# Two deformable convolution layers on one core: gathered tile and tent-sampled half strip issued as one mixed step

## What is computed

```
x = x + relu(bn(deform(gn(x))))                        # layer 0
y = gelu(bn1(deform_masked(gn(x))))                    # layer 1, first convolution
x = x + gelu(bn2(deform_masked(y)) + gn(x))            # layer 1, second convolution
```

## Time and profile before

| | us |
|---|---|
| median of 3 runs | 7444.57 |
| lowest and highest of them | 7428.19, 7445.72 |
| the profiled execution | 7424.53 |
| its span, first to last instruction | 7422.6 |
| mean granted clock of TensorE, share of full | 0.848 |

### The profile page before, as it was taken

The page is one execution under the profiler, slowest core; times in us unless marked ns, Lnnn a source line. Parts: engine busy times, 40 slices in busy tenths (PEclk is TensorE's granted clock), DMA queues, the critical chain, the costliest instruction groups (busy, mean ns, idle before and its releaser), DMA issues. The chain is left out here.

```text
span 7422.6 us, 123328 instructions
## 1 busy us (share of the span) xinstructions
PE 5979.6 (81%) x46325; PEld 4693.6 (63%) x46325; DVE 4858.5 (65%) x11223; ACT 2184.1 (29%) x3355; POOL 5073.7 (68%) x4909
## 2 busy tenths in 40 slices
PE   7985665664878887788887788879999998998997
PEld 6874554553666665566665455547777776776775
DVE  7875666664777675677765455556676775676665
ACT  1221222121222222222222222224444443443442
POOL 0007777777777774777774666767777777777776
PEclk9986777775888887888887788879999998998998
DMA  4322333333333332333331222223333333333332
GB/s 143 99 95 87 93 88 91 92 94 93 99 89 98 89 88 71 89 95 97 103 89 56 76 73 65 62 81 87 91 84 95 88 88 88 91 89 76 93 85 72
DMA packets 366225, 653.49 MB, mean 88 GB/s; under 512 B 113896, under 2 KB 272488, under 8 KB 357736
## 3 DMA queue, kind: packets, MB, share of 16 engines
q0 software_dynamic: 156672, 321.18, 16.9%
q1 hardware_dynamic: 209000, 324.67, 14.2%
HBM read 599.42 MB, written 46.07 MB: 87 GB/s over the span
## 5 line engine op out<-in xcount | busy, mean ns | idle before, releaser
L832 POOL DMA_INDIRECT G<-table,IDX x4896 | 5059.6, 1033 | 2302.9 <-issue 2130.8
L1343 ACT ACTIVATE SAMP<-RED 96x384 f32<-96x384 f32 x1216 | 591.0, 486 | 4357.3 <-PE RED L1049 1327.2
L1981 DVE TENSOR_TENSOR ARENA<-ARENA 128x288 f32<-128x288 f32 x3744 | 1440.6, 451 | 216.7 <-PE RED L1049 207.0
L1049 PE MATMUL RED<-IDENT,ARENA 128*96 128x128 f32 x11232 | 1396.0, 286 | 198.8 <-DVE ARENA L1981 198.8
L1049 PEld LDWEIGHTS RED<-IDENT,ARENA 128*96 128x96 f32 x11232 | 1299.3, 133 | 277.3 <-issue 267.2
L1838 DVE TENSOR_TENSOR G<-G,W 128x1152 f32<-128x1152 f32 x476 | 646.8, 1359 | 603.1 <-DMA G<-table,IDX 598.6
L1034 PE MATMUL RED<-IDENT,SUM 128*96 128x128 f32 x1056 | 242.9, 353 | 745.0 <-DVE SUM L1852 745.0
L1151 PE MATMUL BTP<-PAD,ARENA 80*128 x2304 | 756.9, 452 | 66.7 <-DVE ARENA L1831 32.7
L992 PE MATMUL OFFC<-PAD,ARENA 128*54 128x128 f32 (+1 forms) x10944 | 787.8, 305 | 27.2 <-ACT PAD L1252 15.4
L992 PEld LDWEIGHTS OFFC<-PAD,ARENA 128*54 128x54 f32 (+1 forms) x10944 | 704.7, 140 | 95.7 <-issue 74.0
L1089 PE MATMUL BTP<-X 80*128 80x480 f32 x1152 | 694.2, 735 | 6.5 <-DVE X L1942 4.1
(11 more groups left out here) (201 smaller groups left out, 6175.6 us busy)
## 6 DMA issues: line engine op xcount, KB each, us to landing
ARENA<-wtab SPq DMA_DIRECT2D x208, 800.0 KB
G<-table,IDX POOLq DMA_INDIRECT x4896
ARENA<-xo SPq DMA_DIRECT2D x96, 720.0 KB
table<-TB SPq DMA_DIRECT2D x64, 384.0 KB, 2.5
X<-xo SPq DMA_DIRECT2D x64, 360.0 KB, 3.6
X<-x SPq DMA_DIRECT2D x2, 3200.0 KB, 22.5
out<-X SPq DMA_DIRECT2D x20, 320.0 KB
wtab<-TB SPq DMA_DIRECT2D x16, 384.0 KB, 2.8
```

What stands on the lines that cost most here:

```text
L832: pool.indirect_dma_start(G[:, b, k, :], None, tables[seg.table], bass.IndirectOffsetOnAxis(ap=IDX[:, q, b * TAPS + k:b * TAPS + k + 1], a ...
L1049: last = nc.tensor.matmul(RED[b % 2][0:TPG * C, gr * 128:(gr + 1) * 128], PROD[gr][:, sft, :], IDENT[:, :], start=(sft == 0), stop=(sft == ...
L1343: nc.scalar.activation(SAMP[:, x], RED[x][0:TPG * C, 0:GROUPS * 128].rearrange("p (g n) -> p g n", g=GROUPS), ACT.Copy).then_inc(z.samp_re ...
L1981: last = nc.vector.tensor_tensor(out=PROD[gr][:, :, j * C:(j + 1) * C].rearrange("p (dy dx) c -> p dy dx c", dy=3), in0=win[:, gr:gr + 3, ...
```

## The change

A new kind of step, f, holds a gathered tile and a half strip. It replaces every c and the g beside it: 8 steps in pairs 1 and 2 each, 16 in pair 3. `consume_both` writes its order by hand on SP, PE, ACT and DVE; the tile's projections now go unit by unit (`project_units`), the half reduces into `RED[1]` alone and the tile into `RED[0]` alone. `place` is split into `locate` and `index`, which stand apart. `tents1` works on one image at a time and is called in later units of the step ahead. `MIXED_C` now holds 12 g, 6 f and 26 d (it was 19 g, 6 c, 26 d), and three tiles of a pair, in place of two, come after the norm: f, 5 builds, f, 4 builds, g. POOL's program is as it was.

```diff
-MIXED_C = ("gddgddgc" * 2) * 3 + "gdd"
+MIXED_C = "gddgdfd" * 4 + "gddgddfd" * 2
...
+        def mix(on, c, kinds, gseg, at, dseg, at_d, cseg, at_c, then=""):
...
+                halves = at_c + kinds[:i + 1].count("f")
+                ahead = (cseg, halves) if (kinds + then)[i + 1:i + 2] == "f" else None
...
+                if kind == "f":
+                    k = halves - 1
+                    prep = None
+                    if k % 2 and k + 1 < len(cseg.tiles):
+                        prep = (cseg, k // 2 + 1, 0, c.n, cseg.first // 2 + k // 2 + 1)
+                    half = Step(cseg, k, 0, c.u + 1, c.v, 1 - c.u % 2, cseg.first + k, c.n, prep, (), closes, None, c.wg, False, c.built)
+                    on.consume_both(step, half)
+                    before += ((cseg, k, c.u + 1, 1 - c.u % 2),)
+                    c.n += prep is not None
+                    c.half += 1
...
-                    mix(on, c, MIXED_C, g, 0, DSEG[p + 1], 0, s, 0)
+                    mix(on, c, MIXED_C, g, 0, DSEG[p + 1], 0, s, 0, "f")
                     if p == 2:
                         on.dense_done(c.u)
                     on.norm(3 + p, (p + 1) // 2, (p + 1) % 2, None, c.u)
-                    for k in range(2):
-                        mix(on, c, "gc", g, 19 + k, None, 0, s, 6 + k)
-                        builds_of(on, c, WBUILD[k], KB["t", p + 1], GSEG[p + 1], False)
+                    mix(on, c, "f", g, 18, None, 0, s, 6, "f")
+                    builds_of(on, c, WBUILD[0], KB["t", p + 1], GSEG[p + 1], False)
+                    mix(on, c, "f", g, 19, None, 0, s, 7)
+                    builds_of(on, c, WBUILD[1], KB["t", p + 1], GSEG[p + 1], False)
+                    mix(on, c, "g", g, 20, None, 0, s, 8)
                 else:
                     on.finished(ENDS[0])
-                    for k in range(3):
-                        mix(on, c, "gcgc", g, 2 * k, None, 0, s, 2 * k)
+                    for k, kinds in enumerate(("gf", "ff", "ff")):
+                        mix(on, c, kinds, g, 2 * k, None, 0, s, max(0, 2 * k - 1), "f")
                         builds_of(on, c, range(3 * k, 3 * k + 3), KB["t", PAIRS], GSEG[PAIRS], False)
-                    mix(on, c, "gc" * 10 + "g", g, 6, None, 0, s, 6)
+                    mix(on, c, "f" * 11, g, 6, None, 0, s, 5)
...
+                def consume_both(step, half):
+                    if half.prep:
+                        on.prepare(*half.prep)
+                    if half.t + 1 < len(half.seg.tiles):
                         for im in range(2):
...
+                            load_half(half.seg, half.t + 1, im)
...
+                def consume_both(step, half):
                     for e in tb_evac:
                         pe.wait_ge(e, step.built)
...
+                    for side, e in enumerate(xt1_evac):
+                        pe.wait_ge(e, column_evacs(half.seg.p, side))
+                    tiles = [(b, 0, step.po, b // 2) for b in range(UNITS)]
+                    halves = [(im, 1, half.po, 0) for im in range(2)]
+                    on.taps_half(half, 0, 0)
+                    if step.prep:
+                        on.convolve(*step.prep)
+                    on.taps_half(half, 0, 1)
+                    on.reduce_half(half, 0, 0)
+                    if step.prep:
+                        on.turn_offsets(*step.prep)
+                    on.taps_half(half, 0, 2)
+                    on.turn_unit(step, 0)
+                    on.reduce_half(half, 0, 1)
+                    on.taps_half(half, 1, 0)
+                    on.reduce_half(half, 0, 2)
+                    on.project_units(step, tiles[0:1], 3)
+                    on.turn_unit(step, 1)
+                    on.taps_half(half, 1, 1)
+                    on.reduce_half(half, 1, 0)
+                    on.project_units(step, [tiles[1], halves[0]], 5)
+                    if half.prep:
+                        on.convolve_within(*half.prep)
+                    on.taps_half(half, 1, 2)
+                    on.turn_unit(step, 2)
+                    on.reduce_half(half, 1, 1)
+                    on.project_units(step, tiles[2:3], 6)
+                    on.turn_unit(step, 3)
+                    on.reduce_half(half, 1, 2)
+                    if half.prep:
+                        on.turn_after_tile(*half.prep, step.prep)
+                    on.project_units(step, tiles[3:4], 7)
+                    on.project_units(step, halves[1:2], 8)
...
+                def consume_both(step, half):
+                    def tile_sample(b):
+                        act.wait_ge(main.reduced, UNITS * step.i + b + 1 + 2)
+                        on.sample(step.v + (1, 3, 4, 6)[b], 0)
+
+                    def half_sample(im):
                         act.wait_ge(prod_used, step.wg + 3 * im + 3 + GROUPS)
...
+                        on.sample(step.v + (2, 5)[im], 1)
+
+                    if step.prep:
+                        on.offsets(*step.prep)
+                    tile_sample(0)
+                    if step.prep:
+                        on.mask(*step.prep)
+                    half_sample(0)
+                    tile_sample(1)
+                    if half.prep:
+                        on.offsets(*half.prep)
+                    tile_sample(2)
+                    tile_sample(3)
+                    half_sample(1)
+                    if half.prep:
+                        on.mask(*half.prep)
+                    if step.ahead:
+                        on.tents1(*step.ahead, 0)
+                    on.finish(step, 7)
+                    on.finish(half, 8)
+                    if step.ahead:
+                        on.tents1(*step.ahead, 1)
...
+                def consume_both(step, half):
+                    m, q = step.i, step.q
                     dve.wait_ge(main.prep_v, PREP * step.n)
                     for im in range(2):
...
+                        b = 2 * im
+                        on.weight_half(half, im, 0)
+                        on.scale(main, m, q, b)
+                        on.weight_half(half, im, 1)
+                        on.halve(main, m, b)
+                        on.weight_half(half, im, 2)
+                        on.weight_half(half, im, 3)
+                        on.sum_up(main, m, b)
+                        on.weight_half(half, im, 4)
+                        on.scale(main, m, q, b + 1)
+                        on.weight_half(half, im, 5)
+                        if im == 0:
+                            for tile_ in step.before:
+                                on.finish(*tile_)
+                        on.weight_half(half, im, 6)
+                        on.halve(main, m, b + 1)
+                        on.weight_half(half, im, 7)
+                        on.sum_up(main, m, b + 1)
+                        on.weight_half(half, im, 8)
+                        if im == 0 and step.prep:
+                            on.locate(*step.prep)
                     if step.prep:
...
+                        on.index(*step.prep)
+                        on.weigh(*step.prep)
+                    if half.prep:
+                        on.prepare(*half.prep)
                     if step.closes:
...
+                        for now in (step, half):
+                            on.finish(now.seg, now.t, now.u, now.po)
```

More of the change, by code:

```diff
@@ L384, in loop @@
             with eng.Fori(0, count) as j:
-                before = None
+                before = ()
                 for i, slot_ in enumerate(slots):
@@ new lines, in mix @@
+                prep = seg2 and (seg2, t2, buffer_of(seg2, t2), c.n, seg2.first + t2)
+                step = Step(seg, t, buffer_of(seg, t), c.u, c.v, c.u % 2, seg.first + t, c.n, prep, before, closes,
+                            ahead, c.wg, c.drain, c.built)
+                before = ((seg, t, c.u, c.u % 2),)
+                c.n += prep is not None
[7 more added lines that the diff above has]
+                    before += ((cseg, k, c.u + 1, 1 - c.u % 2),)
+                    c.n += prep is not None
+                    c.half += 1
+                elif kind == "d":
+                    on.consume_dense(step)
+                else:
+                    on.consume(step)
@@ L1069, in reduce_half, with turn_unit @@
                                                 start=(w == 0), stop=(w == WY1 - 1), is_transpose=True)
                     last.then_inc(prod_used, 1)
-                def consume_half(step):
-                    seg, t, prep = step.seg, step.t, step.prep
-                    p, h = seg.p, step.i
-                    r0, _ = column_groups(p)
+                def turn_unit(step, b):
+                    pe.wait_ge(main.summed, UNITS * step.i + b + 1 + UNITS)
+                    pe.wait_ge(main.samp_ready, step.v + (1, 3, 5, 6)[b])
+                    for gr in range(GROUPS):
+                        last = nc.tensor.transpose(RED[0][0:TPG * C, gr * 128:(gr + 1) * 128],
```

(28 more changed lines are left out.)

174 lines of the change are left out of this document (74 added, 100 removed).

## The result

The changed kernel takes **7306.56 us** in the median of 4 runs (7298.02 to 7324.67), the kernel before 7442.59 (4 runs, 7428.19 to 7445.72). The ratio is **0.9824**, with a 95% interval of 0.9801 to 0.9848: 136 us less, where the forecast said 198. The time lies 7 us outside the forecast's own 7200 to 7300 and inside the full range, 7190 to 7370. The profiled execution took 7298.0 us, span 7296.2.

What follows compares the result with a forecast made beforehand. POOL's gather issue was taken as nearly the limit, its 265 us of waits the most to gain. Savings of 157 us before pair 3 plus 55 in pair 3, less 14 at the end, gave 198: 7247 us, range 7190 to 7370.

Steps and rivals of the forecast that it cites:

- f's price, 38 and 42 us: Time of a step f: 38 us plain, 42 where its half prepares the next strip, mean 40, in place of 49.2.
- the rivals with f at 47 and 52: PE waits inside f and its clock falls: f at 47 gives 7363, chance 0.2; at 52 gives 7525, chance 0.09.
- One of their signs: Signs of the slow-f rivals: f steps over 46 us apart, DVE waiting for BTP, and a clock under 0.8.
- Pair 1, norm at 2757.7: In pair 1 the norm's first instruction moves from 2822.2 to 2757.7, 64.5 us less.
- The 6 us allowed for two limits that don't mesh: Added in pairs 1 and 2, where engines and POOL were forecast as equal limits: 6 us of loss each.
- The passage, 120: From the norm's first instruction to the next pair's first gather: parts sum to 119, taken as 120, in place of 132.8.
- Pair 2, 1058 from norm to norm: From pair 1's norm to pair 2's: 1058 us in place of 1136.9, 79 less.
- Pair 3, 45.8 us per tile: POOL's gathering sets pair 3's tiles: 45.8 us each, 782 us in place of 837, 55 less.
- The end, 14 us: Behind pair 3's last gather, the last unit must land and four weightings follow before X is reloaded: 14 us lost.
- The clock: Dense tiles run at granted clock 1.00, against the skill's transpose rule; by that rule f takes 60, kernel some 340 slower.
- The step that failed: In the bound: gathers keep 1118, 1058 and 968 ns in pairs 1 to 3, so POOL's 265 us of waits cap the gain.
- The third rival: Gathers get longer in pairs 1 and 2 because SP's dense windows come closer together: 80 us given back, 7327; chance 0.11.

Runs made afterwards that it cites:

- bursts: Changed kernel, but inside f DVE scales, halves and sums both units of an image in one burst behind its second weighting; 7312.02 us, ratio 0.9862.
- neither instruction: Changed kernel with DVE's scaling and halving of every unit left out, SP's loads kept; 27294.81 us on another chip, including gathers of the general path.
- each part alone: Kernel before with three tiles kept and no f: 7388.88 us. Changed kernel with f but only two tiles kept: 7324.21 us.

## Why the prediction was right, and where it was short

The time lies in the range, on its slower side, and the mechanism was the one forecast: POOL's waits went, and POOL's own issue became the limit. That the forecast's own 7200 to 7300 was missed has one main cause, at the end of this part.

- *f's price, 38 and 42 us.* 38 is right, and if anything high. With two tiles kept the passage ends with the wait for the table; its 116.9 us, less the other parts of the forecast's sum (43), leave 36.9 for each f. The 42 of an f that prepares a strip was not met where the engines set the time. Ahead of the tile beside the norm POOL waits 1.7 us in pair 1 and 4.6 in pair 2 for a unit, and never over 0.3 in pair 3, so f bounds none of them. The clock did not fall (0.86 in pairs 1 and 2, 0.85 in pair 3): the rivals with f at 47 and 52 are out. One of their signs came all the same: in pair 3 the steps are 47.3 us apart, and DVE waits longer for BTP than for G (us in total, times, longest). With POOL never waiting there, f's own waits are no bound.

```profile
DVE ARENA L2031 <- PE BTP L1087: 169.1, 84, 9.5
DVE G L1931 <- DMA G<-table,IDX: 127.9, 32, 9.9
```

- *Pair 1, norm at 2757.7.* It came 983.4 us behind pair 1's start in place of 974.7. The 6 us allowed for two limits that don't mesh should have been 15. One experiment that only changes the order ahead of the norm brings it to 971.4.
- *The passage, 120.* 126.5 and 126.8. Of POOL's forecast gaps of 18, 5 and 5 the first was 29.5, the second 5.1 to 6.4; the table was there in time: with 4.0 us for the store, as in the kernel before, it was ready 9.8 us before POOL came to it, 117 us behind the norm. So the engines kept the forecast's 119 and POOL was late. The tile beside the norm is summed up later than I had it, as its f starts only when the norm is done.
- *Pair 2, 1058 from norm to norm.* 1090.2. Of the 32 us, 28 ns x 756 = 21 are longer gathers and 7 the passage.
- *Pair 3, 45.8 us per tile.* POOL does set it, with nothing else in it, but at 47.3: 41 ns x 612 = 25 us.
- *The end, 14 us.* Half. The wait for the reload ends 28.6 us behind POOL's last gather of pair 3 (before 21.2), the first wait in the second convolution grows from 23.8 to 31.1, and the rest of the kernel only by 4.5.
- *The clock.* The stretch with a granted clock of 1.00 is not made of transposes alone: the reductions against the identity are 64% of PE's busy time in it, offset convolutions and projections 35%. So the full clock of the stretch doesn't tell what transposes alone would be granted. What speaks for it is that 15 of them take 1.80 us in the fast rows and 3.13 in the slow ones.

**The step that failed** is one sentence of the bound: "As the gathers are not changed", 1118, 1058 and 968 ns stay. Measured are 1116, 1086 and 1009 ns, and 46 of the missing 60 us hang on it: the price of a gather was a fixed term, where it goes by what DVE does at its start. The third rival had longer gathers, at 7327, near the 7306.56 measured, but for the wrong reason, SP's windows, and in the wrong pairs: pair 1 stayed at 1116 and pair 3, where the least is moved (70 GB/s against 93), grew most. That a gather's length depends on what DVE runs beside it could be read before: the second convolution, mixed by unit in the same way, already had 1006 ns where pair 3 had 968, and single gathers took up to 4.45 us where nine multiplications stood beside them.

That spreading DVE's work through f raised the hits in pair 3 is supported twice (bursts: 40.4 to 22.5 us; neither instruction: none on another chip). How it does so can be read from where gathers start. In pair 3 of before, 60 gathers start in a scaling (there are 68), none in a halving and 59 in a summing up; in the changed kernel 79, 63 and 18; with bursts inside f 69, none and 66. And a gather that starts in a scaling has 0.15 us of it left in before, 0.39 in the changed kernel (medians). In a burst the scalings are 2.55 us apart. A gather that is held ends 0.82 us behind the scaling and the next starts 0.30 later, at 1.12, with 0.16 us of the summing up left, which costs next to nothing (2.2 us in all). The one after starts some 1.28 later, at 2.40, with 0.15 us of the next scaling left. So in a burst gathers fall into step with DVE and are hardly held; a weighting between two instructions breaks that. This is worked out from these rows; the bursts alone have tested it.

## To carry over

Before an engine's instruction is entered in a sum at a fixed price, look at its shortest and its mean: a gap (here 944 against 968 to 1118 ns) has a cause, and a change of *order* on another engine can move it. When a bottleneck is lifted off one engine (POOL's waits, 127 + 138 us) the next limit is that engine's own issue, and there each 10 ns of an instruction issued 612 times is 6 us. A change made of two parts is tested by each part alone; here they add up, 39 and 97 to 138, but a part's worth can itself hold a shift of phase, as the 39 do.

## What the chip did that I had not expected

- An indirect gather that starts in a DVE instruction with two inputs in SBUF ends 0.81 to 0.83 us behind that instruction (741 of 741 with over 250 ns left); in one with a PSUM input it is not held (0 of 118); a one-input tensor_scalar holds it too, to 0.75 us behind its end (36 of 36). What follows in the row does not matter, but for 46 gathers that started 0.19 to 0.20 us before the end of a multiplication, or 0.31 to 0.32 before that of an addition, and waited for the whole row, up to 4.46 us.
- The same kernel takes 7423 to 7443 us on two occasions and 10862 to 11194 us on three other chips, with equal counts of instructions and, but for PE's and the gathers', equal lengths; there, in pair 3 of the changed kernel, ACT is busy 10% while POOL gathers and 33% while it waits. The change is worth 5.0% on the one of them where it ran and 1.8% here. The cause stays open.
